# An adapter and mixture-of-experts kernel: wider first loads, second expert's weights asked for earlier, third's later, SiLU ahead of a weight split

## The reference, cut to what is computed

```python
# x: (4, 512, 512) float32, adapter_idx: (4,)
base = einsum('bsi,oi->bso', x, W_base)
h = einsum('bsi,ji->bsj', x, Wt)
z = einsum('bsj,brj->bsr', h, A[adapter_idx])
l = einsum('bsr,bor->bso', z, B_w[adapter_idx])
c = base + einsum('bso,po->bsp', l, Wp) * scaling[adapter_idx][:, None, None]
# mixture of experts over 2048 tokens: 16 experts, 2 per token, inner size 352
probs = softmax(c @ gate_w.T)
topk_w, topk_idx = top_k(probs, 2)
topk_w = topk_w / (sum(topk_w) + 1e-20)
hidden = silu(c @ w_gate[e].T) * (c @ w_up[e].T)      # for every chosen expert e
y = sum over the two chosen e of topk_w * (hidden @ w_down[e].T)
out = x + y
```

## Time and profile before

| | us |
|---|---|
| median of 3 runs | 373.61 |
| lowest and highest run | 373.27, 375.55 |
| the profiled execution, its own time | 377.5 |
| its span, first to last instruction | 375.7 |
| PE busy | 355.6 (95%) |
| DVE, ACT, POOL busy | 197.1, 179.1, 130.5 |

### The profile page before, as it was taken

One profiled execution on the slowest core, in us unless ns is written; L12 is line 12 of the kernel. 1 busy time (PEld: TensorE's weight loads), 2 busy tenths in 40 slices (PEclk: granted clock), 3 DMA queues, 4 the chain that ended last, 5 costly groups with the idle time before them and its releaser, 6 DMA issues.

```text
span 375.7 us, 7602 instructions
## 1 busy us (share of the span) xinstructions
PE 355.6 (95%) x2053; PEld 312.9 (83%) x2053; DVE 197.1 (52%) x272; ACT 179.1 (48%) x242; POOL 130.5 (35%) x85
## 2 busy tenths in 40 slices
PE   8899999998789999999999999999999999999980
PEld 4677777787679999999999999999999998888860
DVE  0475699894064627272654826548272655546210
ACT  1468721512165463645547455474555456364320
POOL 0000000021522524564554645546355454232131
PEclk9969999999999999999999999999999999999997
DMA  7990882835887675939297793866948474920422
GB/s 222 398 473 2 308 309 90 317 100 200 307 261 207 186 246 90 336 67 316 39 271 237 219 312 80 263 185 212 313 90 270 109 226 130 301 34 4 55 36 32
DMA packets 29633, 73.78 MB, mean 196 GB/s; under 512 B 3648, under 2 KB 4032, under 8 KB 29504
## 3 DMA queue, kind: packets, MB, share of 16 engines
q1 hardware_dynamic: 20624, 54.30, 41.4%
q0 software_dynamic: 8960, 18.89, 23.1%
HBM read 60.59 MB, written 19.92 MB: 214 GB/s over the span
## 4 chain that ended last, share of the span: by engine, by line
PE 78%; DMA 9%; issue 4%; ACT 2%; SPq 2%; DVE 1%; ACTq 1%; DVEq 1%; POOLq 0%
PE bank L632 33%; PE bank L651 18%; DMA w_raw<-wall 5%; PE bank L505 4%; PE bank L506 4%; PE bank L507 4%; PE bank L566 4%; PE bank L610 3%; PE bank L404 3%; DMA wpt_sb<-wpt 2%; ACT w_hi L335 1%; DMA y_rows<-y_st 1%; PE bank L515 1%; PE bank L433 1%; DMA xg<-y_rows,gidx 1%
## 5 line engine op out<-in xcount | busy, mean ns | idle before, releaser
L1129 POOL DMA_INDIRECT out<-ys,sidx x40 | 73.4, 1835 | 138.5 <-ACT ys L780 77.5
L1112 POOL DMA_INDIRECT xg<-y_rows,gidx x40 | 56.6, 1414 | 99.9 <-issue 88.5
L337 DVE TENSOR_TENSOR w_lo<-w_raw,w_hi (+2 forms) x32 | 76.3, 2385 | 23.8 <-ACT w_hi L335 19.5
L632 PE MATMUL bank<-w_hi,xt_hi 128*128 x320 | 80.7, 333 | 0.2 <-issue 0.2
L632 PE MATMUL bank<-w_lo,xt_hi 128*128 x320 | 77.2, 322 | 0.0
L632 PE MATMUL bank<-w_hi,xt_lo 128*128 x320 | 77.2, 322 | 0.0
L335 ACT ACTIVATE w_hi<-w_raw (+2 forms) x32 | 64.8, 2024 | 6.4 <-issue 2.9
L771 ACT ACTIVATE sg<-bank 128x352 f32<-128x352 f32 x40 | 18.6, 465 | 79.6 <-PE bank L632 74.2
L632 PEld LDWEIGHTS bank<-w_hi,xt_lo 128*128 128x128 f32 x320 | 55.8, 188 | 0.0
L632 PEld LDWEIGHTS bank<-w_lo,xt_hi 128*128 128x128 f32 x320 | 55.6, 188 | 0.1
L632 PEld LDWEIGHTS bank<-w_hi,xt_hi 128*128 128x128 f32 x320 | 53.9, 189 | 1.1 <-issue 1.1
(11 more groups left out here) (171 smaller groups left out, 376.0 us busy)
## 6 DMA issues: line engine op xcount, KB each, us to landing
w_raw<-wall SPq DMA_DIRECT2D x16, 1408.0 KB
w_raw<-wall SPq DMA_DIRECT2D x16, 768.0 KB
x_st<-xt SPq DMA_DIRECT2D x8, 512.0 KB, 12.3
y_rows<-y_st SPq DMA_DIRECT2D x16, 256.0 KB, 3.9
wt_sb<-wt SPq DMA_DIRECT2D x4, 256.0 KB, 4.6
wpt_sb<-wpt SPq DMA_DIRECT2D x2, 512.0 KB, 7.0
wb_sb<-wb SPq DMA_DIRECT2D x2, 512.0 KB, 8.6
wbt_sb<-wbt SPq DMA_DIRECT2D x2, 512.0 KB, 9.5
```

The source lines that it names most:

```text
L337: e.tensor_tensor(w_lo[:, bass.ds(dst, n)], raw, hi, ALU.subtract).then_inc(own, 1)
L632: mm = e.matmul(bank[2 + 2 * s + t % 2][:, 0:INTER], a, w[:, bass.ds(at + (k * GU + s * INTER), INTER)], start=k == 0 and a is hi and w is ...
L1112: e.indirect_dma_start(out=xg[t % NXG][:], out_offset=None, in_=y_dram, in_offset=bass.IndirectOffsetOnAxis(ap=gidx[:, t:t + 1], axis=0)). ...
L1129: e.indirect_dma_start(out=out, out_offset=bass.IndirectOffsetOnAxis(ap=sidx[:, t:t + 1], axis=0), in_=ys[t % NYS][:], in_offset=None, bou ...
```

## The change

The first loads become four: `head` is A of all adapters and the first half of Wt side by side (rows of 5 KB, 640 KB), then the second half of Wt (rows of 4 KB, 512 KB), `head2` is B_w and the first half of Wp (640 KB), then the second half of Wp. The adapter indices ride in the constants. `low_rank` now waits for each half. SP asks for run 1's gu weights after the store of chunk 13, once `v_ohq` is up, so ahead of the stores of chunks 14 and 15. Runs 2 and later wait for the gather of tile 5. ACT, from step 32 on, does the gu split of tile t+2 behind `silu(t)` and `h_evac(t)`.

```diff
+HEAD = KH * RR + KH // 2 * H
+C_SECOND, N_LATE = CH - 3, 5
...
+        head_sb = r_raw1("head_sb", [P, HEAD], F32)
+        wt_sb = r_raw1("wt_sb", [P, KH // 2, H], F32)
+        head2_sb = r_raw1("head2_sb", [P, HEAD], F32)
+        wpt_sb = r_lo0("wpt_sb", [P, KH // 2, H], F32)
+        at_s = head_sb[:, 0:KH * RR].rearrange("p (k r) -> p k r", r=RR)
+        bw_in = head2_sb[:, 0:KH * RR].rearrange("p (k r) -> p k r", r=RR)
...
-            load(at_s[:], at, d_small[0])
-            for k in range(KH):
-                load(wt_sb[:, k], wt[:, k], d_wt[k])
-            load(bw_in[:], bw, d_small[1])
+            load(head_sb[:], head, d_wt[0])
+            load(wt_sb[:], wt, d_wt[1])
+            load(head2_sb[:], head2, d_wpt[0])
+            load(wpt_sb[:], wpt, d_wpt[1])
+            load(cs[:], cst, d_cst)
             for i, half in enumerate(halves):
-                load(wpt_sb[:, half], wpt[:, half], d_wpt[i])
-            load(cs[:], cst, d_cst)
-            load(wb_sb[:, halves[0]], wb[:, halves[0]], d_wb[0])
-            load(wb_sb[:, halves[1]], wb[:, halves[1]], d_wb[1])
-            load(adp_sb[:], adp, d_adp)
+                load(wb_sb[:, half], wb[:, half], d_wb[i])
...
                 e.dma_start(y_dram[c * P:(c + 1) * P, :], y_st[c % NYST][:]).then_inc(d_y[c % NYST], 16)
+                if c == C_SECOND:
+                    e.wait_ge(v_ohq, 1)
+                    load_weights(e, runs, 1, ["gu"])
                 if c == C_LOAD:
                     e.wait_ge(v_tab, 1)
                     runs = table(e, T_REX, T_RUNS, TOPK, NEXP)
                     load_weights(e, runs, 0)
-            for part in PARTS:
-                if part == "gu":
-                    e.wait_ge(v_ohq, 1)
-                else:
-                    e.wait_ge(d_g[1], 16)
-                load_weights(e, runs, 1, [part])
+            e.wait_ge(d_g[1], 16)
+            load_weights(e, runs, 1, ["dn"])
+            e.wait_ge(d_g[N_LATE], 16)
             for r in range(2, NEXP):
                 load_weights(e, runs, r)
...
-            e.wait_ge(d_small[0], 16)
-            low_rank(bank[0][0:RR, :], at_s, wt_sb, d_wt).then_inc(m_p, 1)
+            low_rank(bank[0][0:RR, :], at_s, head_sb, wt_sb, d_wt).then_inc(m_p, 1)
             e.wait_ge(v_bw, 1)
-            low_rank(bank[1][:], bw_s, wpt_sb, d_wpt).then_inc(m_qt, 1)
+            low_rank(bank[1][:], bw_s, head2_sb, wpt_sb, d_wpt).then_inc(m_qt, 1)
...
-                    if t + 2 < NTILE:
+                    if t < NFULL:
                         split_weights(e, count, t + 2, ahead, "gu", a_gu)
                     if t < NTILE:
                         silu(t)
                     if NFULL <= t < NTILE:
                         h_evac(t)
+                    if NFULL <= t < NTILE - 2:
+                        split_weights(e, count, t + 2, ahead, "gu", a_gu)
...
-            e.wait_ge(d_small[1], 16)
+            e.wait_ge(d_wpt[0], 16)
...
-            e.wait_ge(d_adp, 16)
-            step(e.tensor_copy(mask[:], adp_sb[:]))
+            step(e.tensor_copy(mask[:], cs[:, C_IDS:C_IDS + NBATCH].bitcast(I32)))
```

More of the change, by code:

```diff
@@ L80, with build @@
 SKIP = 4096
-C_ID, C_IQ, C_TOK, C_ADP, C_AT, C_BEF, C_TOP, C_RNK, C_SEL, C_SCL, C_GT, CW = (
-    0, P, P + TQ, *(P + TQ + CH + i for i in range(5)), *(P + TQ + CH + 4 + RANK + i for i in (0, P, P + 1, P + 1 + KH * NEXP)))
+C_ID, C_IQ, C_TOK, C_ADP, C_AT, C_BEF, C_TOP, C_RNK, C_SEL, C_SCL, C_GT, C_IDS, CW = (
+    0, P, P + TQ, *(P + TQ + CH + i for i in range(5)),
+    *(P + TQ + CH + 4 + RANK + i for i in (0, P, P + 1, P + 1 + KH * NEXP, P + 1 + KH * NEXP + NBATCH)))
 R_TRI, R_ONE, R_REV, R_THR, R_CUM, R_TH3, R_IM, RW = 0, P, 2 * P, 2 * P + 16, 2 * P + 32, 2 * P + 288, 2 * P + 293, 3 * P + 293
-def build(nc, cst, rcst, at, bw, adp, wt, wpt, wb, wbt, xt, x, wall, out):
+def build(nc, cst, rcst, head, head2, wt, wpt, wb, wbt, xt, x, wall, out):
     with ExitStack() as ctx:
@@ L127, in build @@
         oh_m = region(o_hi + SLOT, KH * SEQ * 4)("oh_m", [P, NSEL, P], BF16)
+        r_raw1 = region(o_raw + SLOT, SLOT)
+        head_sb = r_raw1("head_sb", [P, HEAD], F32)
+        wt_sb = r_raw1("wt_sb", [P, KH // 2, H], F32)
+        head2_sb = r_raw1("head2_sb", [P, HEAD], F32)
         r_lo0 = region(o_lo, SLOT)
-        at_s, bw_in = [r_lo0(n, [P, KH, RR], F32) for n in ("at_s", "bw_in")]
+        wpt_sb = r_lo0("wpt_sb", [P, KH // 2, H], F32)
+        at_s = head_sb[:, 0:KH * RR].rearrange("p (k r) -> p k r", r=RR)
+        bw_in = head2_sb[:, 0:KH * RR].rearrange("p (k r) -> p k r", r=RR)
         bw_s = r_lo0("bw_s", [P, KH, P], F32)
@@ L159, in build @@
         words_f = r_t("words_f", [P, 2], F32)
-        r_raw1 = region(o_raw + SLOT, SLOT)
-        wt_sb = r_raw1("wt_sb", [P, KH, H], F32)
-        wpt_sb = r_raw1("wpt_sb", [P, KH, H], F32)
         r_x = region(o_raw + SLOT, SLOT)
@@ L176, in build @@
         mask, scaled = [r_b(n, [P, NBATCH], F32) for n in ("mask", "scaled")]
-        adp_sb = r_b("adp_sb", [P, NBATCH], I32)
         r_y = region(o_b, KH * H * 4)
@@ L218, in build @@
         y_dram = nc.dram_tensor("y_rows", [NTOK, H], F32, kind="Internal").ap()
-        d_cst, d_rc, d_adp = [sem("d_" + n) for n in ("cst", "rc", "adp")]
+        d_cst, d_rc = sem("d_cst"), sem("d_rc")
         v_bw, v_gt = sem("v_bw"), sem("v_gt")
-        d_small = [sem("d_" + n) for n in ("at", "bw")]
-        d_wt = [sem(f"d_wt{i}") for i in range(KH)]
-        d_wpt, d_wb, d_wbt = [[sem(f"d_{n}{i}") for i in range(2)] for n in ("wpt", "wb", "wbt")]
+        d_wt, d_wpt, d_wb, d_wbt = [[sem(f"d_{n}{i}") for i in range(2)] for n in ("wt", "wpt", "wb", "wbt")]
         d_x = [[sem(f"d_x{b}_{i}") for i in range(2)] for b in range(NBATCH)]
@@ L405, in k_sum, with low_rank @@
                 return mm
-            def low_rank(dst, a, big, landed):
+            def low_rank(dst, a, top, big, landed):
+                rows = [top[:, KH * RR + k * H:KH * RR + (k + 1) * H] for k in range(KH // 2)]
+                rows += [big[:, k] for k in range(KH // 2)]
                 for k in range(KH):
-                    if k * len(landed) % KH == 0:
-                        e.wait_ge(landed[k * len(landed) // KH], 16)
-                    mm = k_sum(dst, [(a[:, k], big[:, k])], first=k == 0, last=k == KH - 1)
+                    if k % (KH // 2) == 0:
+                        e.wait_ge(landed[k // (KH // 2)], 16)
+                    mm = k_sum(dst, [(a[:, k], rows[k])], first=k == 0, last=k == KH - 1)
                 return mm
@@ L832, in _ @@
             halves = [slice(i * KH // 2, (i + 1) * KH // 2) for i in range(2)]
-            e.wait_ge(d_small[1], 16)
+            e.wait_ge(d_wpt[0], 16)
             e.tensor_copy(bw_s[:].rearrange("p k (i r) -> p k i r", i=P // RR),
-                          bw_in[:].unsqueeze(2).to_broadcast([P, KH, P // RR, RR])).then_inc(v_bw, 1)
+                          bw_in.unsqueeze(2).to_broadcast([P, KH, P // RR, RR])).then_inc(v_bw, 1)
             e.wait_ge(d_cst, 16)
@@ L1192 @@
     gt = chunks(get["L0_ffn_gate_w"].T)
-    adp = np.repeat(get["itok_B_0_3"][None, :], P, axis=0)
+    cst[:, C_IDS:C_IDS + NBATCH] = get["itok_B_0_3"][None, :].view(np.float32)
     cst[:, C_SCL] = np.tile(np.repeat(get["L0_cond_scaling"], RANK), P // RR)
     cst[:, C_GT:C_GT + KH * NEXP] = gt.reshape(P, -1)
+    wt, wpt = chunks(get["L0_cond_Wt"]), chunks(get["L0_cond_Wp"].T)
+    head, head2 = [np.concatenate([a.reshape(P, -1), w[:, :KH // 2].reshape(P, -1)], axis=1) for a, w in ((at, wt), (bw, wpt))]
     gu = np.concatenate([get[n].transpose(0, 2, 1).reshape(NEXP, KH, P, INTER) for n in ("L0_ffn_w_gate", "L0_ffn_w_up")], axis=3)
@@ L1201 @@
     arrays = {
-        "cst": cst, "rcst": rcst, "at": at, "bw": bw, "adp": adp,
-        "wt": chunks(get["L0_cond_Wt"]), "wpt": chunks(get["L0_cond_Wp"].T),
+        "cst": cst, "rcst": rcst, "head": head, "head2": head2,
+        "wt": wt[:, KH // 2:], "wpt": wpt[:, KH // 2:],
         "wb": chunks(get["L0_cond_W_base"]), "wbt": chunks(get["L0_cond_W_base"].T),
```

## The result

| | before | after |
|---|---|---|
| median of runs taken in turns on one chip (9 each) | 374.52 us | 378.76 us |
| lowest and highest | 373.27, 377.19 | 375.82, 380.74 |
| the profiled execution's own time, its span | 377.5, 375.7 | 375.93, 374.1 |

The ratio is 1.0099, with a 95% interval from 1.0056 to 1.0142: slower, by about 4 us, and above the forecast range. The profiled execution of after is one of its two fastest. The nine stood at mean granted clocks from 0.973 to 0.991, and the time follows them: 380.74 at 0.973, 375.82 at 0.991. So the trace alone can't say where the 4 us went; it says what each part did.

What follows compares the result with a forecast made beforehand. PE's work bounds 22.5 to 87 and 112 to 306 us; time can change only in the idle elsewhere. Terms -0.6 - 1.9 - 0.7 + 2.3 = -0.9 us gave a 372.7 us median, range 370.0 to 375.6.

Steps and rivals of the forecast that it cites:

- The sum's base: Whole kernel: the difference is formed on the profiled execution of 377.5 us and taken off the median of 373.61.
- part 2: Run 1's gu ahead of stores 14 and 15: store 15 lands sooner, PE's wait for gather 1 shrinks; -1.9 us.
- part 3: Weights of runs 2 and up behind gather 5: less crowding at PE's 1.50 us wait for `xt_lo`; -0.7 us.
- Part 1: Start-up: wider rows land the first loads sooner, so PE's second product starts earlier; -0.6 us, between -1.3 and +0.4.
- My bound of -1.3: Start-up: the most that quicker first loads can gain, PE's full 1.30 us wait for the first half of Wp.
- Part 1's side bet, the clock: Low clock at 18.8 to 25.7 us: a 0.6 us shift may move its return, worth half either way; counted 0.
- The bound of 0: Store 15 and gather 1: no gain if gu moves at 284 GB/s, the store landing at 91.2 us.
- Part 4: Tail: SiLU first saves 1.05 us, but the later split makes an 8.72 us chain, +3.3; sum +2.3 us.
- Rival (a): Tail: the later split hides, so the sum is -4.25 us, 369.4 us; chance 0.15.
- (b): Early parts: rows don't set the rate, store 15 half held, tail costs +2.3; sum +1.5, 375.1 us; chance 0.24.
- (c): Stores behind gu are held, store 15 landing at 95.25 us; sum +5.8, 379.4 us; chance 0.06.
- (d): Start-up by the skill page's transfer rule: first loads land near 7 us; sum -1.6, 372.0 us; chance 0.05.

Runs made afterwards that it cites:

- E5: The whole change again, against before on one chip; ratio 1.0044 (1.0013 to 1.0075).
- E1: Only the first loads in long rows, with the adapter indices in the first table, against before; ratio 0.9981 (0.9957 to 1.0004).
- E4: Only SiLU ahead of ACT's gu weight splits from tile 32, against before; ratio 1.0065 (1.0042 to 1.0088).
- E8: The whole change without the new first loads, against before; ratio 1.0060 (1.0023 to 1.0096).
- E10: Before with run 1's gu weights asked for behind gather 1's landing, like its down weights, against before; ratio 1.0066 (1.0035 to 1.0096).
- E2: Only run 1's gu weights asked for ahead of the store of chunk 14, against before; ratio 1.0026 (1.0001 to 1.0050).
- E11: Before with 40 more waits on PE, on semaphores long reached, ahead of the second product, against before; ratio 1.0037 (1.0015 to 1.0058).
- E18: The whole change with 16 small products on PE ahead of x_turn(1), against before; ratio 1.0026 (0.9997 to 1.0055).
- E3: Only the weights of runs 2 and later put behind tile 5's gather, against before; ratio 1.0002 (0.9979 to 1.0025).
- E9: The new first loads and the later weights behind tile 5's gather, without the other two parts, against before; ratio 0.9966 (0.9949 to 0.9983).
- E14: Before with both gu and down weights of run 1 asked for ahead of the store of chunk 14, against before; ratio 1.0130 (1.0079 to 1.0180).

## Why the prediction was wrong, step by step

**The sum's base.** The forecast was taken off 373.61; before measured 374.52 beside after. 0.9 us of the 6.1 between forecast and median is that. The other 5.1 are the change itself, -0.9 forecast and +4.2 measured. The four parts, each run alone, add up to +2.8: of the 3.7 us up to there part 2 has 2.9 and part 3 0.8. The last 1.4 us stand only in the nine runs (E5: 1.0044, 1.6 us), with their low clocks.

**Part 1, -0.6: the number fits, in part by luck.** The rates rose as I had read from the rows, in the first stretch from 142 to 358 GB/s. B_w and the first half of Wp had landed by 8.1 to 8.4 us in the ten profiles with part 1 and by 9.4 to 10.4 in the ten without: 1.0 to 2.3 us sooner, not 0.8. The 0.4 us for DVE's copy behind them were never lost, since PE was still in its first product; that one now set the start, at 9.66. My bound of -1.3 had forgotten the 9.65 that I had given for its end. The 0.69 us between the two profiles are not firm either: the second product starts at 8.63 to 9.82 with part 1 and at 9.52 to 11.97 without it. E1 gave 0.7 us, with no change inside its interval.

**Part 1's side bet, the clock, counted as 0: failed.** I treated the low stretch of the earlier trace rows as a fixed thing of the start that might move by 0.6 us. The runs show that it isn't tied to a place. It was gone from the first 26 us in all 19 later profiles, and in 13 of them one stood between 91 and 107 us, behind the wait for gather 1 or the next. Part 4 gave it two more places, the idles of 1.7 us in the tail: a stretch stood behind them in the profiles of E4 and E8, though in none of the whole change. It is worth 1.4 to 3.2 us in the nine runs and 0.5 to 0.7 in E5, by the reckoning above. Where the nine had it is not shown, since only one of them has a profile. The range should have held that: the profiled execution of before, 3.9 us over its median, had warned of it.

**Part 2, -1.9: wrong, +1, and the largest term of the miss.** Two steps failed. The first is "2.36 us of this come from what shares the queue: gu, asked for right behind it". A store alone takes 2.0 us, that stands; the other 2.4 are one part of sixteen behind a packet of instructions, and with gu behind gather 1 (E10) it still lands 4.27 us after the copy. The second is "gu's 1.44 MB flow from 83.4 to 87.0 at 403 GB/s". They took 5.5 us instead of 3.6 (80.23 to 85.76, some 260 GB/s), so their bytes were not through when store 15 was issued at 83.45. Stores 14 and 15 queued behind them, 15 parts of store 15 took 4.0 us instead of 2.0, and the packet came later as well. The bound of 0 that I had given reckoned with such a rate, 284 GB/s.

**Part 3, -0.7: the reason failed, the size is open.** I took half of the 1.50 us at `xt_lo` as crowding that part 3 removes. But E1, E2 and E4, without part 3, have no such wait either, E10 and E11 have it without part 3 (1.30 and 2.15 us), and E18 has it with part 3 (2.05 us): part 3 doesn't decide it. It stands where PE's events come late. E3 gives 1.0002 (0.9979 to 1.0025), so anything from -0.8 to +0.9 us, and E9 is 0.6 us better than E1 relative to before; a small gain isn't ruled out.

**Part 4, +2.3: the mechanism right, the size 1.7.** The turn-to-turn chain of 8.72 us measured 8.57 and 8.55, against 7.06 and 7.01. On the other side the turns of tiles 33 and 35 came 1.4 us sooner in sum, not 1.05. Rival (a) is out. What the sum left out is the clock behind the two idles. That E4 measured 2.4 us, near my 2.3, is luck: a shorter chain and a clock term that I hadn't counted.

**The rivals.** (b) is nearest in mechanism: its tail and its held store are what happened, but it had 375.1: it still won 0.9 us by part 2, and it too had no clock term. (c), the nearest in time with 379.4, named the queue; with 1408 KB ahead it costs 1 us, and only E14's 2176 KB come near its 4.1 us (8.36 us less the 4.39 of before). (d) had the first loads landed near 7 us; head2 landed at 8.14 and the last of them at 9.38.

## What to carry to other kernels

Where a store takes longer in one place than elsewhere, look at which of its parts is late before blaming the transfer next to it: here one part of sixteen waited for a packet of TensorE's own instructions. A transfer moved ahead of a store on the same queue is paid for by those of its bytes that still move when the store is issued, so reckon with the rate of that stretch and not with the best one. And a new idle of TensorE of 1.7 us costs more than itself in those executions in which the clock drops behind it; one profile doesn't show how often. Of this change parts 1 and 3 are worth keeping: 0.9966 and 0.9973 in two groups of runs, faster than before by 1.0 to 1.3 us and, across chips, than the whole change by some 3 us.

## What the runs showed that I had not expected

- One 16 KB packet of instructions holds one of 16 parts of a store; that part lands 1.45 to 1.48 us after the packet's end in 11 of 20 profiles, up to 2.5 us behind the other 15, and in some others such a packet holds nothing. Forty waits on semaphores long reached, in an idle place 70 us earlier, moved the packet from 1.1 us after the copy to 2.4 us before it.
- The granted clock of one kernel differs between executions by more than this change's parts are worth: 0.973 to 0.991 in nine runs of after. With (1 - c) x span taken off whole, two measurements that differ by 0.55% agree within 0.1 us; with 0.75 of it, within 0.6.
- PE's semaphore events come up to 5.1 us after the recorded end of their products in the stretch behind the token stage, on some chips, and with them ACT, DVE and the next tile. What is late there was not found.
